# Splitting the score maxima by way of a PSUM bank, and turning them ahead of the value product

## The reference, cut to what matters

```python
q, k, v = heads(layernorm(x) @ Wq.T + bq), heads(ctx @ Wk.T + bk), heads(ctx @ Wv.T + bv)
scores = where(causal, einsum('bhqd,bhkd->bhqk', q, k) * DH ** -0.5, -inf)
x = x + tanh(g_xattn) * (einsum('bhqk,bhkd->bhqd', softmax(scores), v) @ Wo.T + bo)
x = x + tanh(g_ffn) * channel_mix(layernorm(x))     # sigmoid(xr @ Wr.T) * (relu(xk @ Wk.T)**2 @ Wv.T)
```

## Time and profile before

| | |
|---|---|
| median of 3 runs | 1960.36 us (1958.17 to 1960.98) |
| the profiled execution, its own time | 1958.57 us |
| its span, first to last instruction | 1956.8 us |
| TensorE matmuls busy | 1898.7 us, 97% |
| TensorE weight loads | 1471.8 us, 75% |
| VectorE | 1339.0 us, 68% |
| ScalarE | 1088.0 us, 56% |
| GpSimd | 1210.6 us, 62% |
| mean granted TensorE clock | 0.99 of 2.4 GHz |

### The profile page before, as it was taken

How to read it: one execution, slowest core, us unless ns; L and a number is a source line. 1 busy time by engine, 2 the same in 40 slices (tenths; PEclk the granted TensorE clock), 3 DMA queues, 4 the chain that set the end, 5 groups by cost and what they waited for, 6 DMA issues and landing times.

```text
span 1956.8 us, 35230 instructions
## 1 busy us (share of the span) xinstructions
PE 1898.7 (97%) x11136; PEld 1471.8 (75%) x11136; DVE 1339.0 (68%) x3528; ACT 1088.0 (56%) x2059; POOL 1210.6 (62%) x2001
## 2 busy tenths in 40 slices
PE   4899999999999999999999999998989999999999
PEld 3677777777777777777777777776768888888887
DVE  4767767777676777777677677777566665756654
ACT  4555555555555555555555555555565666656562
POOL 4577767777777777767777677777633333434331
PEclk9999999999999999999999999998999999999999
DMA  6454554645545445554545446454223223232321
GB/s 190 104 126 117 140 128 108 163 109 126 126 122 156 118 121 122 136 147 104 143 117 137 122 114 164 112 139 122 72 102 108 87 91 104 75 108 76 108 65 65
DMA packets 128695, 229.66 MB, mean 117 GB/s; under 512 B 18656, under 2 KB 20704, under 8 KB 127616
## 3 DMA queue, kind: packets, MB, share of 16 engines
q1 hardware_dynamic: 128512, 227.43, 43.6%
HBM read 92.06 MB, written 33.59 MB: 64 GB/s over the span
## 4 chain that ended last, share of the span: by engine, by line
PE 75%; DVE 10%; POOL 6%; issue 5%; ACT 3%; DMA 1%; SPq 0%; ACTq 0%; POOLq 0%; DVEq 0%
PE proj_ps L41 12%; PE proj_ps L42 11%; PE proj_ps L43 11%; PE value_ps L1280 7%; PE score_ps L1236 6%; PE prob_ps L1260 5%; PE score_ps L41 3%; PE score_ps L42 3%; PE score_ps L43 3%; DVE score_ps L964 2%; PE sum_ps L1290 2%; DVE split_max L974 2%; PE sum_ps L43 1%; PE sum_ps L42 1%; PE value_ps L42 1%
## 5 line engine op out<-in xcount | busy, mean ns | idle before, releaser
L964 DVE CUSTOM_DVE_ANT_0 score_ps<-score_ps,causal 128x128 f32<-128x128 f32 (+3 forms) x1024 | 487.6, 505 | 284.6 <-PE score_ps L1236 282.9
L619 ACT ACTIVATE probs<-prob_ps 128x512 f32<-128x512 f32 (+1 forms) x768 | 394.3, 527 | 313.8 <-PE prob_ps L1260 179.1
L1236 PE MATMUL score_ps<-k_stack,q_stack 97*128 97x128 f32 (+3 forms) x1024 | 319.2, 353 | 9.0 <-DVE least L964 3.7
L1260 PE MATMUL prob_ps<-q_stack,k_stack 100*128 100x512 f32 (+3 forms) x1024 | 282.5, 317 | 6.1 <-ACT probs L619 4.6
L451 POOL TENSOR_TENSOR prob_sum<-probs 128x384 f32<-128x384 f32 x256 | 259.4, 1013 | 0.0
L1236 PEld LDWEIGHTS score_ps<-k_stack,q_stack 97*128 97x128 f32 x1024 | 188.6, 190 | 83.3 <-issue 30.7
L500 POOL TENSOR_TENSOR kact<-square,kact 128x512 fp32r<-128x512 f32 x64 | 83.9, 1322 | 235.3 <-ACT kact L695 235.3
L454 POOL TENSOR_TENSOR prob_sum<-prob_sum,probs 128x256 f32<-128x256 f32 x256 | 193.9, 758 | 37.3 <-POOL prob_sum L451 0.9
L1260 PEld LDWEIGHTS prob_ps<-q_stack,k_stack 100*128 100x128 f32 x1024 | 192.8, 192 | 28.9 <-issue 6.9
L440 POOL TENSOR_SCALAR_AFFINE_SELECT probs<-probs 128x256 f32<-128x256 f32 x256 | 104.8, 409 | 177.2 <-ACT probs L619 177.2
L444 POOL TENSOR_SCALAR_AFFINE_SELECT probs<-probs 128x256 f32<-128x256 f32 x256 | 106.9, 418 | 103.3 <-ACT probs L619 103.3
(11 more groups left out here) (145 smaller groups left out, 4873.7 us busy)
## 6 DMA issues: line engine op xcount, KB each, us to landing
k_stack<-staged SPq DMA_DIRECT2D x384, 128.0 KB
q_stack<-staged SPq DMA_DIRECT2D x384, 128.0 KB, 3.1
tiles<-in_x SPq DMA_DIRECT2D x16, 1024.0 KB, 5.6
x_io<-in_x SPq DMA_DIRECT2D x16, 1024.0 KB, 7.9
x<-x_io SPq DMA_DIRECT2D x64, 256.0 KB, 3.1
res<-x SPq DMA_DIRECT2D x64, 256.0 KB, 3.7
out_x<-res SPq DMA_DIRECT2D x64, 256.0 KB, 2.0
tiles<-in_ctxT SPq DMA_DIRECT2D x60, 256.0 KB, 4.4
```

The lines of the kernel that those rows point to most:

```text
L619: nc.scalar.activation(probs[:, u % RING, lo:hi], prob_ps[(3 * u + c) % 2][:, 0:hi - lo], ACT.Exp, scale=SCALE).then_inc(exp_done, 1)
L964: nc.vector.tensor_tensor_reduce(out=here, in0=here, in1=causal[:, LATE - P * t:S], scale=-1.0, scalar=3e38, op0=ALU.add, op1=ALU.min, acc ...
L1236: last = nc.tensor.matmul(here[:, at:at + P * (t + 1)], q_stack[n][0:MASK_ROW + 1, j, P * t:P * t + P], k_stack[n][0:MASK_ROW + 1, j, 0:P ...
L1260: last = nc.tensor.matmul(here[:, at:at + width], k_stack[n][0:ROWS, j, P * k:P * k + P], q_stack[n][0:ROWS, j, P * k:S], start=True, stop ...
```

## The change

`split_maxima` first copies the pair's 8 columns of `least` into the first 8 columns of the score bank that the pair's last scores were in and that VectorE has just read. Both parts are then made from that copy: the high part by a copy from PSUM, the low part by a subtraction with one operand in PSUM and one in SBUF. So there are three instructions on VectorE where there were two, with one more semaphore (`max_moved`). TensorE may write that bank again only when the split is done, so `scores(u, 1)` of even u waits for `max_split` too. The turning moves: to the place in front of `values` in the slots that are multiples of 4, and in slot 10 to the place before `scores(i, 1)`, as in the other even slots.

```diff
             def split_maxima(q):
+                here = score_ps[(6 * q + 5) % 2][:, 0:PAIR * T]
                 dve.wait_ge(scores_read, 2 * T * (q + 1))
+                nc.vector.tensor_copy(here, least[:, q % 2, :]).then_inc(max_moved, 1)
+                dve.wait_ge(max_moved, q + 1)
                 if q > 0:
                     dve.wait_ge(max_turned, q)
-                nc.vector.tensor_copy(split_max[:, 0:PAIR * T], least[:, q % 2, :]).then_inc(max_high, 1)
+                nc.vector.tensor_copy(split_max[:, 0:PAIR * T], here).then_inc(max_high, 1)
                 dve.wait_ge(max_high, q + 1)
-                nc.vector.tensor_tensor(split_max[:, PAIR * T:2 * PAIR * T], least[:, q % 2, :],
-                                        split_max[:, 0:PAIR * T].bitcast(F32), ALU.subtract).then_inc(max_split, 1)
+                nc.vector.tensor_tensor(split_max[:, PAIR * T:2 * PAIR * T], here, split_max[:, 0:PAIR * T].bitcast(F32),
+                                        ALU.subtract).then_inc(max_split, 1)
...
                 if u > 0 or c == 2:
                     pe.wait_ge(scores_read, T * u + (-1, 0, 2)[c])
+                if u > 0 and u % 2 == 0 and c == 1:
+                    pe.wait_ge(max_split, u // 2)
...
-            def values(G, q=None):
+            def values(G):
...
-                    if k == 0 and q is not None:
-                        turn_maxima(q)
...
                 if then:
                     probabilities(u, 0)
+                if 2 <= i <= N and i % HG == 0:
+                    turn_maxima(i // 2 - 1)
                 if i % HG == 0 and 0 <= i - VALUES < N:
-                    values((i - VALUES) // HG, i // 2 - 1)
-                elif i == HG:
-                    turn_maxima(i // 2 - 1)
+                    values((i - VALUES) // HG)
                 share(i, b, s, 0)
-                if 2 <= i <= N and i % HG == 2 and s != 10:
+                if 2 <= i <= N and i % HG == 2:
                     turn_maxima(i // 2 - 1)
                 if now:
                     scores(i, 1)
...
-                if 2 <= i <= N and s == 10:
-                    turn_maxima(i // 2 - 1)
```

More of the change, by code:

```diff
@@ L171, in gated_layer @@
         scores_done, scores_read = sem("scores_done"), sem("scores_read")
-        max_high, max_split, max_turned, max_copied = sem("max_high"), sem("max_split"), sem("max_turned"), sem("max_copied")
+        max_moved, max_high, max_split = sem("max_moved"), sem("max_high"), sem("max_split")
+        max_turned, max_copied = sem("max_turned"), sem("max_copied")
         max_stacked = [[sem(f"max_stacked{n}_{a}") for a in range(2)] for n in range(2)]
```

## The result

The kernel after takes 1927.27 us (median of 4 runs, 1925.51 to 1927.88) where the kernel before takes 1959.44 us in the same comparison (4 runs, 1958.17 to 1960.98): a ratio of 0.9833, with a 95% interval of 0.982 to 0.9845. That is 32 us faster. The forecast was 1933 us, from a gain of 26.5 us, with a range of 1923 to 1945.

What follows compares the result with a forecast made beforehand. TensorE, busy 97% of the span, was taken to bound the kernel. Gains of 14.5 + 3.8 + 8.2 = 26.5 us from 1958.57 us give 1932.1, or 1933.9 for the median; forecast 1933 us, range 1923 to 1945.

Steps and rivals of the forecast that it cites:

- TensorE bounds, so what it stops waiting for is the kernel's: Whole kernel: TensorE's matmuls are busy 97% of the span, so a microsecond of TensorE is a microsecond of the kernel.
- The turn inside costs 0.30 us, in front 0.07; 14.5 us: Value blocks: moving 63 turns in front gains 0.23 us each, 14.5 us, with bounds of 4.4 and 20.8 us.
- rival 3: Value blocks: the turn in front makes a full drain, only 4.4 of 14.5 us remain, about 1943 us; chance 0.07.
- The split is 0.58 us and never held: VectorE: the three-step split always lasts 0.58 us, where it was 0.37 undisturbed and up to 2.41.
- The open point, the copy from SBUF to PSUM: First step of the split: no row showed it; taken as 0.17 us, with bounds of 0.17 and 1.19.
- rival 1: Slot 3's split: the first copy is still held by GpSimd, 7.7 us lost, about 1941 us; chance 0.13.
- The split is in time: Value slots: the split ends before the earlier turn wants it, 0.5 us early in slot 4, 1.1 in slot 8.
- Slot 4's lateness, 0.27 us: Slot 4's value block: the turn's lateness of 0.27 us goes in 14 batches, 3.8 us gained.
- Slot 10, 0.55 us: Slot 10, scores to projection: slot 9's shorter split removes 0.55 us of waiting in 15 batches, 8.2 us; bounds 0 and 8.2.
- The new wait of `scores(u, 1)` costs nothing: TensorE before `scores(u, 1)`: the wait stands behind a turn that has waited for the same count, so it costs nothing.
- Rival 2: Later waits, such as slot 7's for an exponent: 7.5 us of the gain is given back, about 1941 us; chance 0.15.
- The three terms: Sum of the turn's move (14.5), slot 4's lateness (3.8) and slot 10's waiting (8.2): 26.5 us.

Runs made afterwards that it cites:

- turn_inside: Kernel after with the turn back between the first four value matmuls and the rest, slot 10 as after: 1942.02 us, ratio 0.9906.
- high_from_sbuf: Kernel after with the high part copied from `least` in SBUF instead of the score bank: 1943.27 us, ratio 0.9907; run once more, 1948.08 us, ratio 0.9941.
- split_only: Kernel before with only the new three-step split, the turning left in its old places: 1943.67 us, ratio 0.9916.
- slot10_back: Kernel after with slot 10's turn put back behind `scores(i, 2)`: 1930.60 us, ratio 0.9851.
- delay3: Kernel after with the split's first copy to the bank made four times over: 1942.88 us, ratio 0.9917.
- move_only: Kernel before with only the turning moved and the old split kept: 1958.54 us, ratio 0.9995.
- pool_later: Kernel before with GpSimd's two residual and bias additions of slot 3 moved to the head of slot 4: 1956.00 us, ratio 0.9981.

## Why the prediction was right, point by point

**TensorE bounds, so what it stops waiting for is the kernel's.** Right: the gains of the slots add up from batch to batch, 26.7 us over batches 1 to 14, and TensorE is still at 97%.

**The turn inside costs 0.30 us, in front 0.07; 14.5 us.** Right: 0.06 measured (from probability to value matmul 384 ns in the median block, against 321 before), 0.24 us a turn, 15.1 us; turn_inside takes 15 us back. The full drain of rival 3 did not come, nor did the turn in front become free.

**The split is 0.58 us and never held.** Right: 0.57, but for one of 0.82 us in the first batch and one of 0.63, in which there are gaps between steps of the usual length. The open point, the copy from SBUF to PSUM, stays between 169 and 172 ns over 128 times, so rival 1 falls. That the copy within SBUF is held by itself, not only the subtraction, is shown by high_from_sbuf.

**The split is in time.** Right: no turn in front of the values of a later batch waits for it. One in the first batch does, 0.31 us.

**Slot 4's lateness, 0.27 us.** Right: 0.28 over the other value slots, in three kernels.

**Slot 10, 0.55 us.** The mechanism was right and the size somewhat small: 0.63, with 0.06 more at the step shown under split_only. slot10_back shows that the place of the turn has next to no part in it. The gap from `scores(10, 1)` to the projection is 0.74 us and not 0.85, because the turn has left that stretch.

**The new wait of `scores(u, 1)` costs nothing.** Right as far as the list of waits after goes: in front of score_ps TensorE waits for VectorE's `least` (4.4 us in all, and 6.9 us for its weight loads) and for DMAs, and never for `split_max`.

**Later waits.** Rival 2 went the other way: the wait of slot 7 in the earlier trace rows got shorter by 0.1 us instead of longer. It did so in split_only and turn_inside as well and in delay3, whose split lasts 1.18 us, but not in move_only or pool_later. So it comes with the new split, not with a shorter one. The traces show the path. The exponent stands on ScalarE behind L566, which waits for the last of a row of small steps on GpSimd, and one of these steps is held while VectorE makes `attn_low`. Before, and then after:

```profile
734.53 0.74 DVE L995 SCALAR_TENSOR_TENSOR attn_low<-inverse,columns,attn_high 128x512 fp32r<-128x512 f32 x1
734.67 0.66 POOL L476 TENSOR_TENSOR newton<-newton 128x4 f32<-128x4 f32 x1
736.80 0.81 ACT L566 ACTIVATE tiles<-tiles,newton 128x512 f32<-128x512 f32 x1 [1.11 <-POOL newton L486]
```

```profile
718.52 0.74 DVE L1000 SCALAR_TENSOR_TENSOR attn_low<-inverse,columns,attn_high 128x512 fp32r<-128x512 f32 x1
718.77 0.55 POOL L479 TENSOR_TENSOR newton<-newton 128x4 f32<-128x4 f32 x1
720.50 0.82 ACT L567 ACTIVATE tiles<-tiles,newton 128x512 f32<-128x512 f32 x1 [1.01 <-POOL newton L487]
```

With one instruction more ahead of it `attn_low` starts 0.17 us later within its slots, and so meets another of GpSimd's steps, which it holds 0.11 us less. That is a chance of the timing, which the prediction did not have.

**The sum.** This is where the 32 us differ from 26.5. The three terms come to 0.92 + 0.27 + 0.55 = 1.74 us a batch, 24.4 us over batches 1 to 14. Measured, the kernel after is 26.7 us further ahead at the start of batch 15 than at that of batch 1 (28.96 - 2.31): 2.3 us more, most of it from slots 10 and 7. The term that was mis-sized most is the first batch, which I had put at 0 beyond its two turns: there the profile shows a gain of 3.1 us. The view of windows for the first 130 us, before and then after; its columns are the stretch, its length, the busy time of PE, PEld, DVE, ACT and POOL with their instructions, the granted clock, the share of the DMA engines and GB/s:

```profile
0.00:130.00 130.00, 100.17 (x537) 74.56 (x538) 75.71 (x213) 63.20 (x109) 70.95 (x126) 0.93 0.55 146
```

```profile
0.00:130.00 130.00, 98.34 (x549) 74.86 (x550) 77.59 (x231) 64.73 (x113) 70.48 (x129) 0.97 0.56 149
```

A stretch at the lower of TensorE's two clocks, 1.2 GHz, from 92.9 to 99.7 us in the trace before, is absent after; the value block of slot 12 of the first batch, most of it inside that stretch, took 5.04 us before and 3.22 after. Before it TensorE had stood 0.83 us for ScalarE and 0.81 us for VectorE in slot 10. The stretch is absent in move_only, split_only, turn_inside, slot10_back and high_from_sbuf, but that does not make it a gain of the change. It is absent in pool_later too, which has the old split and the old place of the turn and yet gains 1.8 us in the first batch; and it is there, from 92.2 to 99.1 us, in the 1950 us execution of high_from_sbuf. The executions of the kernel before differ as well: of those on record beside the experiments, the 12 with a mean granted clock of 0.990 took 1960.5 us on average and the 7 with 0.993 took 1958.0, and the profiled one has 0.990. So some 2 us of the gain that the two profiles show in the first batch may be chance of the profiled execution. At the other end the kernel after gains 3.5 us over the last 15 slots and loses 1.7 behind them; that was not taken apart.

## What to carry to other kernels

Two small instructions on one engine can take 2.4 us instead of 0.4 because of what another engine does, and the trace shows it as their maximum, not their median; look for short steps with a long tail and for what GpSimd runs at that time. A detour through PSUM, one instruction more, made the chain here independent of it; it pays where someone waits for the end of the chain. And two edits can be worth next to nothing and 16 us alone and 32 together: moving the consumer forward only pays when the producer's worst case, in its worst slot, is out of the way.

## What the runs showed that I had not expected

One program had executions of 1932 and of 1950 us (high_from_sbuf), 0.9% apart, and some 12 of these 18 us go with the order in which two engines start within 0.01 us of each other. The kernel before, whose splits in slots 1 and 9 are held too but on starts that lie 0.09 us or more apart, and the kernel after stay within 2.8 and 2.4 us in the comparison above. A step that can be held, and starts within a few nanoseconds of what holds it, adds spread and not only time.

Small steps cost the same to and from PSUM as within SBUF: 0.170 us for SBUF to PSUM, 0.166 for PSUM to SBUF, 0.166 for the subtraction with one operand in PSUM, beside 0.169 for L974 within SBUF.
